# A new order of the steps on every engine, no filler products, and other waits in a sixteen-batch two-layer kernel

## Time and profile before

| | |
|---|---|
| three runs | 1891.52, 1893.15, 1894.34 us (median 1893.15) |
| profiled execution, span | 1890.0 us |
| busy: TensorE, VectorE | 1668.7 us (88%), 1503.1 us (80%) |
| busy: ScalarE, GpSimd | 1020.8 us (54%), 931.3 us (49%) |
| mean granted TensorE clock | 0.963 of full |
| chain that ended last | TensorE 49%, VectorE 26%, GpSimd 9%, ScalarE 6% |

### The profile page before, as it was taken

The page is one execution under the profiler, slowest core; times in us unless marked ns, Lnnn a source line. Parts: engine busy times, 40 slices in busy tenths (PEclk is TensorE's granted clock), DMA queues, the critical chain, the costliest instruction groups (busy, mean ns, idle before and its releaser), DMA issues.

```text
span 1890.0 us, 34255 instructions
## 1 busy us (share of the span) xinstructions
PE 1668.7 (88%) x12162; PEld 1083.8 (57%) x12269; DVE 1503.1 (80%) x3386; ACT 1020.8 (54%) x1998; POOL 931.3 (49%) x1120
## 2 busy tenths in 40 slices
PE   2466799999999999999999999999999999999876
PEld 1234357565665657565665657565665657565635
DVE  3776879899797979899797979799897979782712
ACT  3243374746556474746556474747556474736252
POOL 4545263646455473646455464637455464632202
PEclk9787799999999999999999999999999999999897
DMA  3001010010101010110102010100102010101000
GB/s 101 0 6 51 7 48 11 25 34 10 55 8 52 13 52 7 34 30 13 52 8 57 8 51 10 36 25 16 48 8 57 8 51 8 39 13 36 22 13 6
DMA packets 66924, 53.39 MB, mean 28 GB/s; under 512 B 8322, under 2 KB 65474, under 8 KB 66754
## 3 DMA queue, kind: packets, MB, share of 16 engines
q1 hardware_dynamic: 63202, 49.55, 9.5%
q10 hardware_dynamic: 3552, 1.65, 0.3%
HBM read 8.44 MB, written 4.19 MB: 7 GB/s over the span
## 4 chain that ended last, share of the span: by engine, by line
PE 49%; DVE 26%; POOL 9%; ACT 6%; issue 4%; SPq 2%; DMA 2%; ACTq 0%; DVEq 0%; POOLq 0%; another core or an unknown queue 0%
PE bank L908 47%; DVE rmax L731 6%; DVE wkb L678 3%; POOL rstd L351 3%; PE bank L904 3%; ACT prob L491 2%; DVE tree L641 2%; DVE stats L632 2%; DVE rmax L728 1%; ACT xd L497 1%; POOL inner L395 1%; DVE prob L811 1%; DMA qh<-part 1%; SPq L325 1%; DVE inner L641 1%
## 5 line engine op out<-in xcount | busy, mean ns | idle before, releaser
L491 ACT ACTIVATE prob<-bank 128x512 f32<-128x512 f32 x640 | 358.6, 596 | 113.8 <-PE bank L908 109.2
L731 DVE TENSOR_REDUCE rmax<-bank 128x1 f32<-128x512 f32 (+2 forms) x768 | 355.1, 505 | 17.9 <-PE bank L908 17.8
L908 PE MATMUL bank<-kh,qh 72*128 72x512 bf16 (+3 forms) x1024 | 264.5, 308 | 28.4 <-DVE rmax L731 20.3
L439 POOL TENSOR_TENSOR prob<-xdT,spread 128x512 f32<-128x512 f32 x128 | 168.0, 1313 | 234.0 <-ACT spread L491 206.6
L908 PE MATMUL bank<-qh,kh 75*128 75x512 bf16 (+3 forms) x1024 | 255.3, 305 | 18.9 <-ACT prob L491 15.7
L908 PE MATMUL bank<-wexpT,prob 128*128 128x128 f32 x2048 | 267.0, 278 | 2.3 <-POOL prob L439 0.7
L908 PEld LDWEIGHTS bank<-wexpT,prob 128*128 128x128 f32 x2048 | 250.0, 192 | 8.9 <-POOL prob L439 0.9
L491 ACT ACTIVATE spread<-bank 128x512 f32<-128x512 f32 x128 | 76.3, 596 | 298.3 <-PE bank L908 244.6
L678 DVE RECIPROCAL wkb<-wkb 128x512 f32<-128x512 f32 x64 | 211.6, 3327 | 0.0
L908 PEld LDWEIGHTS bank<-qh,kh 75*128 75x128 bf16 x1024 | 100.2, 98 | 190.0 <-ACT prob L491 115.8
L347 POOL TENSOR_TENSOR var<-mv,eps_ln 128x4 f32<-128x4 f32 x112 | 33.1, 296 | 339.3 <-DVE mv L637 339.3
(11 more groups left out here) (211 smaller groups left out, 3395.8 us busy)
## 6 DMA issues: line engine op xcount, KB each, us to landing
qh<-part SPq DMA_DIRECT2D x288, 64.0 KB
kh<-part SPq DMA_DIRECT2D x288, 64.0 KB
x<-in_L_attn_x_dram SPq DMA_DIRECT2D x16, 256.0 KB, 2.8
out_dram<-yo SPq DMA_DIRECT2D x16, 256.0 KB, 3.1
qh<-maxT SPq DMA_DIRECT2D x16, 48.0 KB
wk<-in_L_attn_tm_Wk_dram ACTq DMA_DIRECT2D x1, 256.0 KB
wv<-in_L_attn_tm_Wv_dram ACTq DMA_DIRECT2D x1, 256.0 KB
wr<-in_L_attn_tm_Wr_dram ACTq DMA_DIRECT2D x1, 256.0 KB
```

Source lines behind the costliest of these rows:

```text
L439: raised(pool.tensor_tensor(ug[:, e % 4, :], xdT[:, :], spread[e // 2 % 2][:, :], ALU.mult), "ug_side")
L491: raised(act.activation(dst, src, func, **kw), signal)
L731: last = dve.tensor_reduce(rmax[:, j, h:h + 1], S[n % 2][:, col:col + (j + 1) * P], AX_X, ALU.max)
L908: return pe.matmul(out_, w, x, start=start, stop=stop, **kw)
```

## The change

ORDER gets new lists for all engines but SyncE. The four filler steps and all their functions go. In steps with several waits the one put first is now another (`until` on the input ahead of the one that frees the output; on GpSimd, in weigh and in back the order is turned too), and waits that an earlier step of the same engine has already made are left out. ScalarE's helper `move` gets an argument `freed` for the waits on the output's place. The computation stays as it was.

```diff
         2:heads0 2:heads1 0:load 2:max_rows 4:store
     """,
     pool="""
-        0:root0 4:u3 1:r_sig0 4:u5 4:u7 4:u9 4:u11 4:u13 1:wk0 4:u15 1:gated0 1:r_sig1 1:rwkv0 4:root7 1:wk1 1:wk2 2:root_rms 1:r_sig2 1:gated1 1:rwkv1
-        1:gated2 1:wk3 2:rope_sum0 2:rope_sum1 2:rest0 1:r_sig3 1:gated3 1:rwkv2 2:part_lo0 1:rwkv3 2:rest1 2:part_lo1 1:root2 0:x1_gain 0:x1_bias 2:root4
-        1:res 0:root1 3:root6 1:cmr_sig 1:cmr_sum 3:gate_rest 3:gate_lo 1:root3 3:u1
+        296:rwkv1 296:r_sig3 296:gated3 297:rope_sum0 296:wk3 297:rest0 296:rwkv2 297:part_lo0 296:rwkv3 297:rope_sum1 297:rest1 295:root0
+        297:part_lo1 296:root2 295:x1_gain 295:x1_bias 296:res 299:root7 295:root1 298:root6 297:root4 296:cmr_sig 296:cmr_sum 298:gate_rest
+        298:gate_lo 298:u1 298:u3 296:root3 298:u5 295:wk0 298:u7 298:u9 298:u11 295:r_sig0 295:gated0 298:u13 298:u15 295:rwkv0 295:wk1 295:r_sig1
+        295:r_sig2 295:wk2 295:gated1 296:root_rms 295:gated2
     """,
     act="""
-        4:route_exp 2:cmk_tanh3 3:norm4 2:cmr_tanh 1:norm1 4:gate_hi 4:gate_mid 1:mix_before0 4:gT_out 1:mix_before1 1:mix_before2 4:spread1 3:vaug
-        2:norm3 4:spread3 2:xbT_out 1:k_exp0 1:r_tanh0 2:gate0 4:spread5 2:gate1 4:spread7 4:spread9 4:spread11 1:k_first0 1:k_exp1 1:r_tanh1 4:spread13
...
-        3:exp21 3:exp22 1:k_first3 3:exp23 3:exp24 3:exp25 1:r_tanh3 3:exp26 3:exp27 2:part_hi0 3:exp28 3:exp29 2:part_hi1 3:exp30 2:part_mid0 3:exp31
-        3:exp32 3:pvT_out0 3:exp33 3:exp34 3:exp35 3:exp36 3:exp37 2:part_mid1 3:exp38 3:exp39 0:norm0 3:pvT_out1 1:norm2 3:attT_out 1:mix_before3
-        1:mix_before4 1:cmk_tanh0 2:values 3:norm6 1:cmk_tanh1 3:xdT_out 1:cmk_tanh2
+        140:exp24 140:exp25 139:part_hi0 140:exp26 140:exp27 140:exp28 139:part_mid0 140:exp29 140:exp30 140:exp31 140:exp32 140:exp33 139:part_hi1
+        140:exp34 140:pvT_out0 140:exp35 139:part_mid1 140:exp36 140:exp37 140:exp38 140:exp39 137:norm0 140:pvT_out1 138:norm2 140:attT_out
+        138:mix_before3 138:mix_before4 141:norm7 138:cmk_tanh0 138:cmk_tanh1 140:norm6 138:cmk_tanh2 140:xdT_out 140:route_exp 138:cmk_tanh3
+        139:values 138:cmr_tanh 137:norm1 139:norm4 140:gate_hi 140:gate_mid 140:gT_out 137:mix_before0 137:mix_before1 140:spread1 137:mix_before2
+        140:spread3 140:spread5 138:norm3 137:k_exp0 140:spread7 138:xbT_out 137:k_first0 140:spread9 137:r_tanh0 138:gate0 138:gate1 140:spread11
...
     """,
     dve="""
-        0:moments0 3:rowmax18 1:clamp0 3:rowmax19 3:rowmax20 1:kv0 4:u4 3:rowmax21 1:ksum0 3:rowmax22 3:rowmax23 1:kvsum0 2:tree0 3:rowmax24 3:rowmax25
-        4:u6 2:tree1 3:rowmax26 3:rowmax27 3:rowmax28 3:rowmax29 4:u8 3:rowmax30 1:clamp1 3:rowmax31 3:rowmax32 4:u10 2:tree2 3:rowmax33 1:wkv0 3:rowmax34
-        4:u12 3:rowmax35 2:tree3 3:rowmax36 3:rowmax37 4:u14 3:rowmax38 3:rowmax39 3:max_parts 1:inverse0 2:tree4 1:clamp2 1:kv1 2:tree5 2:tree6 2:tree7
-        1:ksum1 4:yd 4:moments7 1:kvsum1 1:wkv1 1:clamp3 1:kv2 1:ksum2 1:kvsum2 2:yb 2:moments4 1:inverse1 1:wkv2 1:kv3 1:kvsum3 1:ksum3 1:wkv3
-        2:rope_mul0 2:rope_mul1 2:rope_mul2 2:rope_mul3 1:inverse2 1:inverse3 1:x2 1:moments2 3:attend0 3:attend1 0:moments1 3:yc 1:mix3 3:moments6
-        2:rowmax0 2:rowmax1 1:mix4 2:rowmax2 2:rowmax3 1:silu0 1:silu1 2:rowmax4 1:silu2 3:route_logits 2:rowmax5 3:route_probs 1:silu3 3:largest0
-        2:rowmax6 3:others 2:rowmax7 3:largest1 2:rowmax8 3:gates 2:rowmax9 1:y0 2:rowmax10 2:rowmax11 2:rowmax12 1:moments3 3:u0 2:rowmax13 0:mix0
-        2:rowmax14 2:rowmax15 0:mix1 0:mix2 2:rowmax16 3:u2 2:rowmax17
+        178:rowmax3 178:rowmax4 177:silu0 178:rowmax5 178:rowmax6 177:silu1 178:rowmax7 178:rowmax8 177:silu2 178:rowmax9 179:route_logits
+        178:rowmax10 179:route_probs 177:silu3 179:largest0 179:others 178:rowmax11 178:rowmax12 179:largest1 179:gates 178:rowmax13 178:rowmax14
+        177:y0 178:rowmax15 178:rowmax16 179:u0 177:moments3 178:rowmax17 179:u2 178:rowmax18 176:mix0 178:rowmax19 176:mix1 178:rowmax20 176:mix2
+        179:u4 178:rowmax21 178:rowmax22 176:clamp0 179:u6 178:rowmax23 178:rowmax24 176:ksum0 178:rowmax25 178:rowmax26 179:u8 176:kv0 178:rowmax27
+        178:rowmax28 178:rowmax29 178:rowmax30 176:kvsum0 178:rowmax31 178:rowmax32 179:u10 177:tree0 176:wkv0 178:rowmax33 178:rowmax34 177:tree1
+        178:rowmax35 179:u12 178:rowmax36 178:rowmax37 176:clamp1 179:u14 178:rowmax38 178:rowmax39 178:max_parts 177:tree2 176:inverse0 177:tree3
+        176:kv1 176:clamp2 177:tree4 177:tree5 177:tree6 177:tree7 176:kvsum1 176:wkv1 179:yd 176:ksum1 176:kv2 176:clamp3 176:kvsum2 176:wkv2
+        176:ksum2 177:yb 177:moments4 176:inverse1 176:kv3 176:kvsum3 176:ksum3 176:wkv3 177:rope_mul0 177:rope_mul1 176:inverse2 176:inverse3
+        177:rope_mul2 177:rope_mul3 175:moments0 179:moments7 176:x2 176:moments2 178:attend0 178:attend1 177:rowmax0 177:rowmax1 175:moments1
+        177:rowmax2 178:yc 176:mix3 178:moments6 176:mix4
     """,
     pe="""
-        4:expert15 1:r2 3:score0 3:score1 1:v2 3:score2 3:score3 2:leafT0 3:score4 3:score5 1:k3 3:score6 3:score7 2:leafT1 3:score8 3:weigh0 3:score9
-        3:score10 3:weigh1 3:weigh2 3:score11 3:score12 2:leaf_sum 3:score13 3:weigh3 3:score14 3:score15 1:r3 3:score16 3:score17 1:v3 3:score18 3:weigh4
-        3:score19 3:weigh5 3:score20 3:weigh6 2:xcT 3:score21 3:weigh7 3:score22 2:rope0 3:score23 2:rope1 3:score24 3:score25 2:rope2 2:rope3 3:score26
-        3:score27 3:score28 3:score29 3:weigh8 3:score30 3:weigh9 3:weigh10 3:score31 3:score32 3:weigh11 3:score33 3:score34 3:back0 3:score35 3:score36
-        3:score37 1:read_out0 1:read_out1 3:score38 1:read_out2 3:score39 1:read_out3 3:weigh12 3:weigh13 3:weigh14 3:weigh15 2:attn_v 3:back1
-        2:busy_rows0 3:attT 1:xn2T 3:attn_out 2:busy_rows2 2:row0 2:row1 1:cmk0 3:busy_experts2 2:row2 2:row3 1:cmk1 2:row4 3:xdT 1:cmk2 2:row5
-        3:centroids 1:cmk3 2:row6 3:shared 1:cmr 1:cmv0 2:row7 2:row8 1:cmv1 2:row9 1:cmv2 1:cmv3 2:row10 3:busy_gates1 2:row11 0:xnT 2:row12 3:gT 2:row13
-        2:row14 3:gb0 3:biases 3:gb1 2:row15 3:expert0 2:row16 3:gb2 2:row17 3:expert1 1:xbT 0:k0 0:v0 2:row18 3:gb3 2:row19 3:expert2 2:row20 3:gb4 0:r0
-        2:row21 1:gates0 3:gb5 1:gates1 2:row22 2:row23 3:expert3 2:row24 2:row25 3:gb6 3:expert4 3:expert5 2:row26 0:k1 3:gb7 2:row27 2:row28 3:gb8
-        2:row29 3:expert6 2:row30 2:row31 3:gb9 3:expert7 2:row32 3:gb10 3:expert8 2:row33 3:gb11 2:row34 0:r1 2:row35 3:gb12 3:expert9 3:gb13 2:row36
-        2:row37 3:expert10 3:gb14 2:row38 2:row39 3:expert11 3:gb15 0:k2 0:v1 2:maxT 3:expert12 3:expert13 3:expert14
+        230:score12 229:leaf_sum 230:score13 230:weigh3 230:score14 230:score15 228:v3 230:score16 230:score17 228:r3 230:score18 230:score19
+        230:weigh4 230:weigh5 230:score20 229:xcT 230:weigh6 230:score21 230:score22 229:rope0 229:rope1 230:score23 230:weigh7 230:score24
+        230:score25 229:rope2 230:score26 230:score27 229:rope3 230:score28 230:weigh8 230:score29 230:score30 230:weigh9 230:weigh10 230:score31
+        230:score32 230:weigh11 230:score33 230:score34 228:read_out0 230:score35 228:read_out1 228:read_out2 230:score36 230:back0 230:score37
+        228:read_out3 230:score38 230:score39 230:weigh12 230:weigh13 230:weigh14 230:weigh15 230:back1 229:row0 229:row1 230:attT 228:xn2T 229:row2
+        230:attn_out 229:attn_v 229:row3 229:row4 228:cmk0 228:cmk1 229:row5 229:row6 228:cmk2 229:row7 229:row8 230:xdT 229:row9 230:centroids
+        229:row10 228:cmk3 229:row11 228:cmr 229:row12 230:shared 228:cmv0 228:cmv1 229:row13 228:cmv2 229:row14 228:cmv3 229:row15 230:gT 229:row16
+        227:xnT 230:gb0 230:biases 229:row17 230:gb1 230:expert0 230:gb2 229:row18 229:row19 230:gb3 230:expert1 229:row20 230:gb4 230:expert2
+        229:row21 227:v0 229:row22 227:k0 230:gb5 230:expert3 230:gb6 229:row23 229:row24 230:expert4 230:gb7 229:row25 228:xbT 229:row26 230:gb8
+        230:expert5 229:row27 227:r0 229:row28 230:gb9 230:expert6 229:row29 230:gb10 229:row30 228:gates0 229:row31 229:row32 228:gates1 230:expert7
+        229:row33 229:row34 227:k1 230:gb11 230:expert8 229:row35 230:gb12 229:row36 230:expert9 229:row37 230:gb13 230:expert10 230:gb14 229:row38
+        229:row39 230:expert11 230:gb15 227:v1 227:r1 229:maxT 230:expert12 230:expert13 230:expert14 227:k2 230:expert15 229:score0 229:score1
+        227:r2 229:score2 229:score3 227:v2 229:score4 229:score5 228:leafT0 228:leafT1 229:score6 229:score7 227:k3 229:score8 229:score9 229:weigh0
+        229:score10 229:weigh1 229:weigh2 229:score11
     """,
 )
 
...
                 until(pool, b, "r_sig", c + 1)
-                until(pool, b, "wkv", c + 1)
                 raised(pool.tensor_tensor(rth[:, c % 2, :], rth[:, c % 2, :], kvb[:, c % 2, :], ALU.mult), "gated")
 
             def weighted(b, c):
+                until(pool, b, "wk_inv", c + 1)
                 until(pool, b, "gated", c + 1)
-                until(pool, b, "wk_inv", c + 1)
```

(54 more changed lines are left out.)

77 lines of the change are left out of this document (25 added, 52 removed).

## The result

| | before | after |
|---|---|---|
| median of the runs, four of each on one chip | 1893.02 us (1891.52 to 1894.34) | 1795.63 us (1795.06 to 1800.05) |
| ratio | | 0.9494 [0.948, 0.9507] |
| span of the profiled execution | 1890.0 us | 1794.2 us |
| period, from maxT to maxT | 105.64 us | 99.99 us |
| back1 to gT, first part | 23.49 | 21.99 (-1.50) |

The account below looks back on a forecast made before the run. Neither TensorE nor VectorE is full: latency rules back1 to gT, and TensorE becomes the bound from gT to maxT. Terms 0+0-2.2-0.2-0.2 = -2.6 us a period, x 14.5 = 37.7, give 1855.4 us; range 1818 to 1902.

Parts of the forecast that it names:

- 14.5 periods: Multiplier for the gain per period: 13 full periods, plus 1.5 for the fill and the drain's three shorter periods.
- First part: back1 to gT, 23.49 us: latency rules, so it stays as long but does more; value 0, ends -1.7 and +1.1.
- Second part: gT to maxT, 34.90 us: VectorE loses 4.9 us of work, TensorE 1.2; value -2.2, ends 0 and -4.9.
- TensorE becomes the bound: gT to maxT: TensorE sets the time, with 1.2 us less work and 1.0 us of waits dropped.
- Score phase: maxT to back1, 47.25 us: nearly unchanged as TensorE's waits absorb added work; value -0.2, ends +0.9 and -1.5.
- I take 1.06 of them as filled: Score phase: of 6.8 us of TensorE's waits for exponentials a period, 1.06 are filled by added work.
- x2's wait: VectorE's 6.3 us before x2 cover moved moments and rope products, which would cost 4.0 us without that cover.
- Fillers: Eight TensorE products a batch between back1 and gT, 1.7 us in all; removing them valued 0, end of gain 1.7.
- Waits: Dropped wait instructions on TensorE's queue, 21 x 0.051 = 1.07 us at most; value -0.2 a period, ends 0 and -1.1.
- The second: Rival: the part from gT to maxT follows VectorE, -4.9, with -0.4 from the rest; 1816 us, chance 0.10.
- The third: Rival: row0, ahead of attT and xn2T, waits for SyncE's transfers; slower, 1908 us at a 3.6 us wait; chance 0.10.
- The fourth: Rival: without fillers the clock falls to half in the loose stretch from back1 to gT; 1926 us, chance 0.05.

Follow-up runs that it names:

- e3: The new order without fillers, with all waits as in the kernel before; 1791.95 us, ratio 0.9476.
- i2: The changed kernel with VectorE's rowmax0 and rowmax1 behind moments1 instead of ahead of it; 1829.4 us, ratio 0.9665.
- e4: The changed kernel with the four filler steps put back; 1807.22 us, ratio 0.955.
- h2: The changed kernel with ScalarE's and TensorE's waits in their old form, GpSimd's as new; 1805.15 us, ratio 0.9544.
- g6: The changed kernel with VectorE's moments0 moved from before x2 back to just behind rowmax18; 1810.4 us, ratio 0.9568.
- h3: The changed kernel with VectorE's tree1 moved ahead of rowmax33 and rowmax34, right behind wkv0; 1793.21 us, ratio 0.9472.
- h1: The changed kernel with GpSimd's waits alone (four steps) in their old order; 1781.87 us, ratio 0.9419.
- g8: The changed kernel with attn_v alone moved back in front of back1 on TensorE; 1801.15 us, ratio 0.952.
- e1: The kernel before with the four filler steps taken out of TensorE's list and nothing else; 1901.74 us, ratio 1.0051.
- i3: The old order with fillers and the wait edits of TensorE and ScalarE, GpSimd's waits old; 1885.12 us, ratio 0.9954.
- g7: The changed kernel with row0, row1 and row2 put behind attT, xn2T, attn_out and attn_v on TensorE; 1874.58 us, ratio 0.9909.

## Why the forecast was right in sign and 60 us off in size

The forecast counted 2.6 us a period over 14.5 periods, 37.7. The spans differ by 95.8: 44.2 of the missing 58.1 are 3.05 us a period more (x 14.5), and 13.9 are the fill, the drain and the number of periods.

The missing 3.05 us by part: 1.50 in the first, 0.84 in the second, 0.91 in the score phase, less the 0.2 that the forecast gave to the waits and that lie inside the parts here. With the wait edits taken apart (e3) it looks otherwise: the order alone brought 1.5 for a forecast of 0, 2.5 for 2.2 and 2.2 for 0.2, and the wait edits cost 0.5 where a gain of 0.2 was forecast. Two steps failed, the 0 of the first part and the 0.2 of the score phase.

- **First part, valued 0 (ends -1.7 and +1.1): -1.50.** This is the step that failed in kind. VectorE's rows were counted right: thirteen units' maxima at its gates step, two of them into the 1.79 us before moments1 (on TensorE it is ten rows ahead of the centroid product, not eleven). But "this part stays as long but does more" took the norms' chain for fixed while VectorE's idleness was filled. i2 shows that the filled wait is worth its length, 1.30 us, and 0.23 more by row2's wait: maxima that aren't done in the wait are done behind it, where the chain through yc and mix3 waits for VectorE. Three more things changed in this part, and their shares of the 1.50 overlap. With the fillers put back it is 22.65 (e4), so 0.66 needs their absence. x2 starts 3.24 us ahead of back1 before and 3.74 after, and moments1 comes 3.04 us behind back1 before and 2.55 after. And the old order's blocked routing step (0.77 us for 0.23, above) is free in the new one.
- **Second part, -2.2 (ends 0 and -4.9): -3.04.** Near in size: 0.5 of it is TensorE's and ScalarE's wait edits (32.37 in e3 and h2, 31.86 in after), 2.5 the order. "TensorE becomes the bound" is half true: of 1.29 us more work for VectorE 1.01 comes through (g6), of 0.84 less only 0.5 (h3), so in the new order the two engines are within a few tenths of each other here, and the part ends where both are full. In after it also carries 1.0 us of tree1's lock-out, of which 0.5 counts.
- **Score phase, -0.2 (ends +0.9 and -1.5): -1.11,** inside the ends only by an accident: the order alone gave -2.2 (e3, and h1 without the blocked tree step, both 45.05), outside them, and GpSimd's wait edit took 1.1 back. This is the term furthest off. That TensorE sets most of this phase was right: before x2 VectorE still waits 3.8 us, and attn_v's place is worth nothing (g8). Its start is not TensorE's: the blocked tree step there, 1.1 us of VectorE's, lengthened the phase by 1.1 in both orders, through clamp2 and ScalarE. What failed is "I take 1.06 of them as filled": more is gone than the added projection takes. The last exponential ends 43.72 us behind maxT before and 42.83 in e3, and from there to back1 it is 3.53 us before, with read_out3 and attn_v in it, and 2.22 in e3, with neither. Which of the moved steps does it was not tested, so the cause of these 2.2 us stays open.
- **x2's wait.** "If it went they would cost 4.0 us" was never called on: 3.8 us of that cover are left.
- **Fillers, 0: right** for the path (e1 at full clock 105.65), wrong as a whole: their worth was the clock, and they cost 0.6 us a period where rows have taken their place (e4).
- **Waits, -0.2 (ends 0 and -1.1).** Net +0.5 to +0.6 in both orders, outside the ends. TensorE's and ScalarE's edits gain 0.4 to 0.5 (i3, h2), within them. The sentence that putting the latest wait first "changes the order of such instructions, not their number" missed that it changes when GpSimd starts, by 0.09 us, and whom it meets. The forecast read the earlier trace rows for TensorE's queue alone.
- **14.5 periods: too few.** The last two intervals gained 4.8 and 4.7 us, nearly as much as a full one, and the stretch up to the first maxT 9.3.
- **Rivals.** The second (-5.3 a period, 1816 us), the one nearest to the result, got 0.10. Its sum is near by luck: it put the gain into the second part (-4.9), and the runs spread it over three. The third did not come: row0 starts without a wait for transfers. The fourth did not come in after (clock 1.00 over the whole period) but its mechanism is real: e1 shows it in the old order, i2 and g7 in the new one as soon as rows come a little later.

## What to carry to other kernels

Where an engine with an ordered list waits on a latency chain, put work that is ready into that wait. Here it was worth the wait's length (1.30 us) because that engine's work set what followed, though the stretch looked bound by latency. Then do the same count for the engine that is next to full, as it decides how much of the relief comes through, and ask which steps of other engines wait for the work that is moved. A move can't be valued apart from the rest of the order: the same step gave 0.3 us in one and 1.0 in the other. Look at the spread of one instruction's durations, not at its mean: 0.17 and 1.27 us for the same step is a collision, and a tenth of a microsecond on the other engine removes or makes it.

## What the runs showed of the hardware

- A VectorE scalar_tensor_tensor step on two tensors in SBUF (128x8, 128x16 or 128x64) that starts while a GpSimd tensor_tensor runs lasts until that one ends: 1.2 to 1.3 us for 0.16 to 0.23. So does a tensor_tensor step on two of them (128x64, 0.77 us for 0.23). Maxima read from PSUM (0.68 us) and reciprocals with one input (3.3 us) kept their durations beside the same GpSimd products. The Trainium skill, "SBUF — State Buffer", section SBUF: two separate sides, says that VectorE and GpSimd share a pair of ports as an exclusive lock, which a VectorE instruction with two SBUF inputs takes too, so that the later one is held for the whole instruction. By that rule the traces agree, with 1.27 us here.
- The order of two waits ahead of a GpSimd instruction moved its start by 0.09 us (idle 2.35 and 2.44 us), although the later signal was the same one.
- The granted clock fell to half (for 6.7 and 3.4 us) in some periods of e1 and i2 and not in their neighbours, for the same instructions in the same order and behind the same waits of TensorE, at a price of 1.9 and 1.1 us.
